# A residual add folded into the weights: the identity is added to W on chip, and the two halves of each result are copied out by two engines

## The reference

```
base   = x @ W.T                              # 512 -> 512
logits = x @ Wr.T + 5 * one_hot(sequence id)  # 8 experts
topw, topi = top_k(logits, 2);  weights = softmax(topw)
gates  = weights scattered to the 8 experts
h      = x @ A.T                              # 8 experts x 16
out    = x + base + 2 * sum_e gates_e * (h_e @ B_e.T)
```

## Time and profile before

| | |
|---|---|
| median of 3 runs | 83.89 us (83.81 to 84.14) |
| profiled execution, first to last instruction | 82.0 us |
| PE busy | 76.8 us, 94% |
| DVE, ACT, POOL busy | 48.0, 23.5, 22.6 us |
| chain that ended last | PE 87%, DMA 5% |

### The profile page before, as it was taken

One profiled execution on the slowest core, in us unless ns is written; L12 is line 12 of the kernel. 1 busy time (PEld: TensorE's weight loads), 2 busy tenths in 40 slices (PEclk: granted clock), 3 DMA queues, 4 the chain that ended last, 5 costly groups with the idle time before them and its releaser, 6 DMA issues.

```text
span 82.0 us, 1637 instructions
## 1 busy us (share of the span) xinstructions
PE 76.8 (94%) x504; PEld 72.6 (89%) x504; DVE 48.0 (59%) x218; ACT 23.5 (29%) x60; POOL 22.6 (28%) x26
## 2 busy tenths in 40 slices
PE   5966999999999999999999999999999999999950
PEld 2225999999999999999999999999999999999930
DVE  0027618777475564839282738475564979788650
ACT  6329606333050323123141314050403123111200
POOL 4340420861406060605023231406060606000000
PEclk9999579999999999999999999999999999999999
DMA  1899969628903963999995000180000018033033
GB/s 23 224 280 347 191 173 402 288 33 339 390 18 96 390 282 57 387 420 352 300 420 240 0 0 0 45 339 0 0 0 8 0 48 336 6 122 128 0 128 128
DMA packets 4755, 14.22 MB, mean 173 GB/s; under 512 B 656, under 2 KB 2448, under 8 KB 4496
## 3 DMA queue, kind: packets, MB, share of 16 engines
q1 hardware_dynamic: 4752, 14.17, 49.2%
HBM read 9.98 MB, written 4.19 MB: 173 GB/s over the span
## 4 chain that ended last, share of the span: by engine, by line
PE 87%; DMA 5%; SPq 1%; DVE 1%; ACT 1%; issue 0%; DVEq 0%
PE heads_ps L395 42%; PE base_ps L395 29%; PE heads_ps L421 5%; DMA wh_sb<-in_w_heads 5%; PE base_ps L421 5%; PE heads_ps L425 2%; PE base_ps L425 2%; PE ghT_ps L412 2%; SPq L159 1%; DVE wh_lo L348 1%; ACT wh_hi L251 1%; DVE out_sb L328 1%; SPq L164 1%; DVEq L49 0%
## 5 line engine op out<-in xcount | busy, mean ns | idle before, releaser
L211 POOL TENSOR_TENSOR x_lo<-xT_sb,x_hi 128x512 fp32r<-128x512 f32 x14 | 18.6, 1325 | 40.3 <-ACT x_hi L237 40.3
L395 PE MATMUL heads_ps<-wh_hi,x_hi 128*128 128x392 f32 x64 | 23.4, 366 | 1.2 <-ACT wh_hi L251 1.2
L395 PE MATMUL heads_ps<-wh_lo,x_hi 128*128 128x392 f32 x64 | 22.2, 348 | 0.1
L395 PE MATMUL heads_ps<-wh_hi,x_lo 128*128 128x392 f32 x64 | 22.1, 345 | 0.0
L395 PE MATMUL base_ps<-wb_hi,x_hi 128*128 128x256 f32 x64 | 18.7, 293 | 0.0
L395 PE MATMUL base_ps<-wb_lo,x_hi 128*128 128x256 f32 x64 | 18.4, 288 | 0.0
L395 PE MATMUL base_ps<-wb_hi,x_lo 128*128 128x256 f32 x64 | 18.4, 287 | 0.0
L395 PEld LDWEIGHTS heads_ps<-wh_hi,x_hi 128*128 128x128 f32 x64 | 12.2, 191 | 2.8 <-issue 2.2
L241 ACT ACTIVATE ghT_hi<-ghT_ps 128x128 fp32r<-128x128 f32 x16 | 4.4, 278 | 34.7 <-PE ghT_ps L412 34.7
L283 DVE TENSOR_TENSOR ghT_lo<-ghT_ps,ghT_hi 128x128 fp32r<-128x128 f32 x16 | 4.7, 292 | 15.7 <-ACT ghT_hi L241 15.6
L395 PEld LDWEIGHTS heads_ps<-wh_lo,x_hi 128*128 128x128 f32 x64 | 12.2, 191 | 0.6 <-DVE wh_lo L348 0.6
(11 more groups left out here) (41 smaller groups left out, 91.6 us busy)
## 6 DMA issues: line engine op xcount, KB each, us to landing
x_sb<-in_x SPq DMA_DIRECT2D x4, 768.0 KB, 6.3
out<-out_sb SPq DMA_DIRECT2D x4, 768.0 KB, 4.5
xT_sb<-in_xT SPq DMA_DIRECT2D x3, 768.0 KB, 4.6
xT_sb<-in_xT SPq DMA_DIRECT2D x1, 1024.0 KB, 6.3
x_sb<-in_x SPq DMA_DIRECT2D x1, 1024.0 KB, 9.3
wh_sb<-in_w_heads SPq DMA_DIRECT2D x4, 196.0 KB, 3.9
out<-out_sb SPq DMA_DIRECT2D x3, 256.0 KB, 2.0
xT_sb<-in_xT SPq DMA_DIRECT2D x4, 128.0 KB, 2.9
```

The source lines that it names most:

```text
L211: nc.gpsimd.tensor_tensor(x_lo[s][:, :], xT_sb[:, t, :], x_hi[s][:, :].bitcast(FP32), ALU.subtract).then_inc(x_lo_made, 1)
L395: return nc.tensor.matmul(dst, xs[s][:, k * P:(k + 1) * P], ws[n % 2][:, k, :], start=(k == 0 and n == 0), stop=(k == KC - 1 and n == 2))
```

## The change

- The second copy of the input, `x_sb`, its five loads and their waits are gone.
- The identity is added to the weights instead, in place: output 256 + c of the heads half gets feature 256 + c, which is in chunks 2 and 3 of `wh_sb`; output c of the base half gets feature c, in chunks 0 and 1 of `wb_sb`. Four adds of 128x128 on DVE do that, before ACT makes the upper part of that chunk.
- The heads half of a result is copied out by ACT (`out_rest`), the base half by DVE (`out_base`, now a copy in place of an add). PE's `tile_ready` and SP's stores wait for both.

```diff
+            def out_rest(t, s):
+                act.wait_ge(lora_heads_done, t + 1)
+                nc.scalar.activation(out_sb[:, t, BASE:O], heads_ps[s][:, 0:REST], ACT.Copy).then_inc(heads_read, 1)
...
             for k in range(KC):
                 act.wait_ge(wh_landed[k], 16)
+                if k >= KC // 2:
+                    act.wait_ge(wh_eye_added, k - KC // 2 + 1)
                 nc.scalar.activation(wh_hi[:, k, :], wh_sb[:, k, :], ACT.Copy).then_inc(wh_hi_made, 1)
                 if k == 0:
                     half_upper(0, 1)
             for k in range(KC):
                 act.wait_ge(wb_landed[k], 16)
+                if k < KC // 2:
+                    act.wait_ge(wb_eye_added, k + 1)
                 nc.scalar.activation(wb_hi[:, k, :], wb_sb[:, k, :], ACT.Copy).then_inc(wb_hi_made, 1)
...
                 exponential(t)
+                out_rest(t - 1, (j - 1) % SLOTS)
...
-            def out_rest(t, s, landed, count):
-
-                dve.wait_ge(lora_heads_done, t + 1)
-                dve.wait_ge(landed, count)
-                nc.vector.tensor_tensor(out_sb[:, t, BASE:O], heads_ps[s][:, 0:REST], x_sb[:, t, BASE:O],
-                                        ALU.add).then_inc(heads_read, 1)
-
             def out_base(t, s):
                 dve.wait_ge(lora_base_done, t + 1)
-                nc.vector.tensor_tensor(out_sb[:, t, 0:BASE], base_ps[s][:, 0:BASE], x_sb[:, t, 0:BASE],
-                                        ALU.add).then_inc(out_made, 1)
+                nc.vector.tensor_copy(out_sb[:, t, 0:BASE], base_ps[s][:, 0:BASE]).then_inc(out_made, 1)
...
+            def eye_added(w, k, col, landed, added):
+                dve.wait_ge(landed[k], 16)
+                nc.vector.tensor_tensor(w[:, k, col:col + P], w[:, k, col:col + P], ident[:, :],
+                                        ALU.add).then_inc(added, 1)
+
+            dve.wait_ge(ident_made, 1)
+            for k in range(KC):
+                if k >= KC // 2:
+                    eye_added(wh_sb, k, (k - KC // 2) * P, wh_landed, wh_eye_added)
                 dve.wait_ge(wh_hi_made, k + 1)
                 nc.vector.tensor_tensor(wh_lo[:, k, :], wh_sb[:, k, :], wh_hi[:, k, :].bitcast(FP32),
                                         ALU.subtract).then_inc(wh_lo_made, 1)
+            for k in range(KC // 2):
+                eye_added(wb_sb, k, k * P, wb_landed, wb_eye_added)
             for k in range(KC):
...
                 if not (isinstance(t, int) and t < SLOTS):
+                    pe.wait_ge(heads_read, t - SLOTS + 1)
                     pe.wait_ge(out_made, t - SLOTS + 1)
```

More of the change, by code:

```diff
@@ L34, with cond_resid_program @@
 GROUPED = GROUPS * SLOTS
-def cond_resid_program(nc: bass.Bass, xT: bass.AP, x: bass.AP, ids: bass.AP, w_heads: bass.AP,
+def cond_resid_program(nc: bass.Bass, xT: bass.AP, ids: bass.AP, w_heads: bass.AP,
                        w_base: bass.AP, b: bass.AP, out: bass.AP):
@@ L60, in cond_resid_program @@
         xT_sb = sb("xT_sb", [P, TILES, KC * P])
-        x_sb = sb("x_sb", [P, TILES, D])
         out_sb = sb("out_sb", [P, TILES, O])
@@ L102, in cond_resid_program @@
         xT_group = sem("xT_group")
-        x_group = sem("x_group")
         xT_last = sem("xT_last")
-        x_last = sem("x_last")
         wh_landed = [sem(f"wh_landed{k}") for k in range(KC)]
@@ L116, in cond_resid_program @@
         bias_made = sem("bias_made")
+        wh_eye_added = sem("wh_eye_added")
+        wb_eye_added = sem("wb_eye_added")
         wh_hi_made = sem("wh_hi_made")
@@ L176, in _ @@
             load(xT_sb, xT, 3, SLOTS, xT_group)
-            load(x_sb, x, 0, SLOTS, x_group)
             with sp.Fori(0, GROUPS - 2) as g:
                 sp.wait_ge(xT_group, 16 * g + 16)
-                sp.wait_ge(x_group, 16 * g + 16)
                 load(xT_sb, xT, SLOTS * g + 3 + SLOTS, SLOTS, xT_group)
-                load(x_sb, x, SLOTS * g + SLOTS, SLOTS, x_group)
-            sp.wait_ge(x_group, 16 * (GROUPS - 1))
-            load(x_sb, x, GROUPED - SLOTS, SLOTS, x_group)
             load(xT_sb, xT, GROUPED, TILES - GROUPED, xT_last)
-            load(x_sb, x, GROUPED, TILES - GROUPED, x_last)
             with sp.Fori(0, GROUPS) as g:
+                sp.wait_ge(heads_read, SLOTS * g + SLOTS)
                 sp.wait_ge(out_made, SLOTS * g + SLOTS)
@@ L190, in _ @@
             for t in range(GROUPED, TILES - 1):
+                sp.wait_ge(heads_read, t + 1)
                 sp.wait_ge(out_made, t + 1)
@@ L276, in _ @@
             ghT_upper(TILES - 2, (TILES - 2) % SLOTS)
+            out_rest(TILES - 2, (TILES - 2) % SLOTS)
             ghT_upper(TILES - 1, (TILES - 1) % SLOTS)
+            out_rest(TILES - 1, (TILES - 1) % SLOTS)
         @block.vector
@@ L322, in gated, with step @@
                     ALU.mult, ALU.mult).then_inc(gh_made, 1)
-            def out_rest(t, s, landed, count):
-                dve.wait_ge(lora_heads_done, t + 1)
-                dve.wait_ge(landed, count)
-                nc.vector.tensor_tensor(out_sb[:, t, BASE:O], heads_ps[s][:, 0:REST], x_sb[:, t, BASE:O],
-                                        ALU.add).then_inc(heads_read, 1)
             def out_base(t, s):
                 dve.wait_ge(lora_base_done, t + 1)
-                nc.vector.tensor_tensor(out_sb[:, t, 0:BASE], base_ps[s][:, 0:BASE], x_sb[:, t, 0:BASE],
-                                        ALU.add).then_inc(out_made, 1)
-            def step(t, j, landed, count):
+                nc.vector.tensor_copy(out_sb[:, t, 0:BASE], base_ps[s][:, 0:BASE]).then_inc(out_made, 1)
+            def step(t, j):
                 s, before = j % SLOTS, (j - 1) % SLOTS
@@ L342, in step @@
                 gated(t, s)
-                out_rest(t - 1, before, landed, count)
                 out_base(t - 1, before)
+            def eye_added(w, k, col, landed, added):
[3 more added lines that the diff above has]
+            dve.wait_ge(ident_made, 1)
             for k in range(KC):
+                if k >= KC // 2:
+                    eye_added(wh_sb, k, (k - KC // 2) * P, wh_landed, wh_eye_added)
                 dve.wait_ge(wh_hi_made, k + 1)
@@ L366, in _ @@
                 for j in range(1, 1 + SLOTS):
-                    step(SLOTS * g + j, j, x_group, 16 * g + 16)
+                    step(SLOTS * g + j, j)
             for t in range(GROUPED + 1, TILES - 2):
-                step(t, t, x_last, 16)
+                step(t, t)
             t0, t1, t2 = range(TILES - 3, TILES)
@@ L376, in _ @@
             gated(t1, s1)
-            out_rest(t0, s0, x_last, 16)
             out_base(t0, s0)
@@ L382, in _ @@
             gated(t2, s2)
-            out_rest(t1, s1, x_last, 16)
             out_base(t1, s1)
             ghT_lower(t2, s2)
-            out_rest(t2, s2, x_last, 16)
             out_base(t2, s2)
@@ L518 @@
         "in_xT": np.ascontiguousarray(tokens.transpose(3, 1, 2, 0)).reshape(P, TILES, KC * P),
-        "in_x": np.ascontiguousarray(tokens).reshape(P, TILES, D),
         "in_ids": np.ascontiguousarray(np.asarray(itok_B_0_7).reshape(SEQS, 1)),
```

## The result

The changed kernel took 86.22 us (median of 4 runs, 85.59 to 86.72), the kernel before 84.02 us beside it (83.81 to 84.14). The ratio is 1.026, with a 95% interval of 1.020 to 1.033: slower by 2.2 us where 86.0 was forecast.

The account below looks back on a forecast made before the run. PE's row of matmuls was taken to bound the kernel, with only start and tail open. 82.0 + 2.1 (start) + 0 + 0 = 84.1, plus 1.9 to the median gives 86.0 us; range 84.8 to 86.6.

Parts of the forecast that it names:

- What bounds the kernel: Whole kernel: PE busy 76.8 of 82.0 us, a row of matmuls; only the start and the tail are open.
- The relay: Start: the adds make ACT and DVE wait in turn for wh and wb parts; first half of x_hi 2.7 us late.
- floor of +1.1 us: Start: heads of tile 1 at 12.80 instead of 11.68 from late x_lo, if PE's clock is full by about 12.
- the sum: 82.0 + 2.1 start + 0 steady state + 0 tail = 84.1; with 1.9 us to the median, 86.0.
- a sign of being wrong: Start: the prediction would be wrong if, among other signs, the clock took another course ahead of 8.0 us.
- its fall at 8.03: Start: PE's clock low from 8.03 to 11.43 as before, staying low longer because 8 matmuls with gaps replace 15 without.
- the upper end: Start: low clock lasts as long again, to 14.83; heads of tile 1 lose 0.58 more, +2.56 in all.
- two stretches of the earlier trace: PE's start: clock fell after 9 matmuls with gaps, rose after 15 without a gap.
- Steady state and tail: Per tile: slack 2.5 us, cost nothing, pace 4.39 us; tail: SP's issue holds it, gain nothing to 0.05 us.
- The clock back at once: Rival, start: clock full at about 11.4 as before, cost 1.1 us, 85.0 (84.8 to 85.3); chance 0.33.
- the start absorbed: Rival, start: the 1.6 us by which tile 1's x_lo was early take up the ping-pong; 83.9, chance 0.08.
- ACT late in the steady state: Rival, each of 13 tiles: copy and x_hi use up the 2.5 us slack, PE waits; 89 to 91, chance 0.05.

Follow-up runs that it names:

- The adds alone: Kernel before with only the four 128x128 identity adds and ACT's waits for them put in: 86.18 us, ratio 1.027.
- the change without them: Changed kernel without the four identity adds, so x is missing from the result: 83.80 us, ratio 0.998.
- both copies on DVE: Changed kernel with both result copies on DVE, one behind the other, none on ACT: 86.55 us, ratio 1.026.
- PE kept busy: Changed kernel with 12 filler matmuls of 512 columns on zeros, into an unread bank, in PE's waits in the start: 84.66 us, ratio 1.008.
- kernel before with early ids, kept busy: Kernel before with 4 filler matmuls, the ids' load issued by ACT at its start, and x_hi of tile 2 ahead of b_hi: 83.45 us, ratio 0.986.
- A full clock in it: Kernel before with 4 matmuls on zeros in PE's wait for chunk 1 of wh: 83.99 us, ratio 1.000.
- x_hi of tile 1 ahead of wb_hi: Changed kernel with ACT making x_hi of tile 1 before wb_hi: 86.91 us, ratio 1.037.

## Why the prediction was right

- **What bounds the kernel** held: the steady state kept its 4.39 us per tile, and the whole difference arises in the start. The adds alone cost as much as the change, and the change without them nothing.
- **The relay.** Forecast was 4.19 us from wh_hi 1 to wb_hi 0 (10.21 - 6.02), measured 4.28. An add took 0.28, forecast 0.29. The hand-over from DVE's add back to ACT took 0.10 us (7.09 to 7.19), where I had 0.03. x_lo of tile 1 began at 11.76; forecast, less the 0.26 us by which this run's weights landed sooner, 11.69.
- **Floor and clock.** Forecast was a floor of +1.1 us for the full clock. With PE kept busy it measured +0.7. The steps of the relay were sized right: from wh_hi 1 (5.65 in that run) to the heads of tile 1 (12.56) it was 6.91 us, forecast 6.78. A good part of the difference is the landing: in that trace wh_hi 1 starts 0.37 us sooner than in the trace before. The rest stays open. That the clock would be late as well was right, and it is the bigger part: 1.5 us between the change and the change kept busy, where the sum had 2.1 - 1.1 = 1.0.
- **Where the clock fell** was off, and already ahead of 8.0 us, which the prediction had named as a sign of being wrong. In the trace before, the third matmul of tile 0 had its full-clock time (0.34 us at 5.18); in the one after it had not (0.53 us at 5.41), although the change has done nothing yet at that point. So the clock's course differed from the start, and the forecast, which built on its fall at 8.03, was right in its size and not in its course. The low stretch came from 9.3 to 16.1 in the traced run, not from 8.0 to 13.7 or 14.8. It is as long as the upper end had it, twice 3.4, but later, and falls on denser work: heads of tile 1 begin +2.08 later (forecast +1.98), tile 2 at 19.39 (+3.15 on 16.24, both by the chain in order of time), tile 3 at 23.77 (+2.97 on 20.80), and the span is 2.9 us longer, where +2.56 was my upper end. That traced run was the slowest of the four, and at 86.72 us outside my range; the spans of the four were 84.9, 84.7, 83.8 and 84.1, so the forecast of 84.1 lies among them, and that the median came out so near to it owes something to the spread. What sets the instant at which the clock changes, from run to run, stays open.
- **Gaps and the clock.** That gaps on PE bring the full clock later was my estimate from two stretches of the earlier trace rows. The change kept busy agrees in direction: with the relay unchanged and filler work in the waits, the full clock, once there at about 5.6 us, didn't fall again, and 1.56 us came back. Two other traces don't. In the kernel before with early ids, kept busy, the first three fillers had low-clock times themselves (1.50 us). And in the change without the adds PE waits 1.09 us for chunk 1, as it waits 1.18 in the kernel before, and the clock stays full: 0.34 us for 392 columns at 8.17, where the kernel before has 0.53 at 8.33. So no run shows a rule by which the work on PE sets its clock.
- **The start before.** I said that PE was held there by its own work at the low clock. That is true of the wait at 11.68, but I took it for the only bound. The second floor, the gates that wait for the ids and x_lo of tile 2 behind them, stood just behind it, hidden, and so the low clock of before was free. A full clock in it brought nothing (ratio 1.000).
- **Steady state and tail** were costed at nothing, and measured so: slack 2.35 us (forecast 2.5), tail -0.04 (0 to -0.05). The copy on ACT took 0.385, forecast 0.40.
- **The rivals.** The clock back at once did not occur in the traced run, nor was the start absorbed; ACT late in the steady state was excluded by the pace and by both copies on DVE.

## What to carry to other kernels

Work that is taken off engines which nobody waits for brings nothing, and four adds of 0.28 us cost 2.2 us because each stood between two engines that had run side by side, and because the gaps that this left on PE went with a low clock (some 1.5 of the 2.2 us): price a new dependence by the chain that it closes, not by its instructions. Put such preparation on an engine that is idle and needs nobody's result, here POOL, though it took 1.23 us for two of the adds where DVE took 0.48. And before a stall is mended, look for the wait that stands behind it: in the kernel before, the low clock, the input of tile 1 and the second floor lay within a microsecond or so of one another, and mending the clock alone showed nothing.

## What the runs showed of the hardware

- DVE or POOL took longer in some stretches in which both read two inputs from SBUF. Two adds of 128x128 on DVE took 0.48 us with POOL idle (the changed kernel) and 1.56 beside POOL's subtraction (x_hi of tile 1 ahead of wb_hi), over three times as long. The other way round, POOL's subtraction of 128x512 took 1.77 us in the kernel before beside DVE's b_lo, and 1.29 in the steady state.
- The granted clock that the profile shows doesn't always agree with the duration of the matmuls at the start. With the adds alone, the stretch from 4.4 to 13.3 us reads 1.00, and the matmuls in it take their low-clock times until 13.3. Nor does the 1.00 at the start of the changed kernel's trace fit its first three matmuls, the third of which took 0.53 us. I read the clock from the duration of one matmul that stands behind another: 0.53 or 0.34 us for 392 columns, 0.41 or 0.28 for 256.
- One load more at the very start, of 0.5 KB, came with a later landing of the first weights (ACT starts wh_hi 0 at 4.7 to 4.8 us and not at 3.7) in the traces of all three kernels that had it.

The stretch of PE with the adds alone (length, busy us and count, clock, DMA share and GB/s), and behind it that kernel's PE timeline:

```profile
4.40:13.30 8.90, 8.05 (x23) 1.00 0.93 277
```

```profile
13.07 0.41 PE L411 MATMUL base_ps<-wb_hi,x_lo 128*128 128x256 f32 x1
13.29 0.38 PE L411 MATMUL base_ps<-wb_hi,x_hi 128*128 128x256 f32 x1
13.50 0.28 PE L411 MATMUL base_ps<-wb_lo,x_hi 128*128 128x256 f32 x1
```
